# One matmul of 512 queries per value head instead of two of 256, and a new order of TensorE's work in the attention step

## What is computed

```python
Q = (x @ Wq).reshape(B, S, NUM_HEADS, 2 * HEAD_DIM).transpose(0, 2, 1, 3)
K = (x @ Wk).reshape(B, S, NUM_HEADS, 2 * HEAD_DIM).transpose(0, 2, 1, 3)
V = (x @ Wv).reshape(B, S, NUM_HEADS, HEAD_DIM).transpose(0, 2, 1, 3)
Q1, Q2 = jnp.split(Q, 2, axis=-1)
K1, K2 = jnp.split(K, 2, axis=-1)
A1 = jnp.einsum('bhqd,bhkd->bhqk', Q1, K1) * scaling
A2 = jnp.einsum('bhqd,bhkd->bhqk', Q2, K2) * scaling
attn = jax.nn.softmax(A1, axis=-1) - lamb * jax.nn.softmax(A2, axis=-1)
out = jnp.einsum('bhqk,bhkd->bhqd', attn, V)
```

## Time and profile before

| | us |
|---|---|
| median of three runs | 3233.75 (3232.12 to 3233.81) |
| span of the profiled execution | 3232.2 |
| TensorE busy | 3089.3 |
| VectorE busy | 2735.8 |
| ScalarE busy | 2502.6 |
| attention steps with all three kinds of work | 193.8 to 2487.7 |

### The profile page before, as it was taken

The page is one execution under the profiler, slowest core; times in us unless marked ns, Lnnn a source line. Parts: engine busy times, 40 slices in busy tenths (PEclk is TensorE's granted clock), DMA queues, the critical chain, the costliest instruction groups (busy, mean ns, idle before and its releaser), DMA issues. The chain is left out here.

```text
span 3232.2 us, 72457 instructions
## 1 busy us (share of the span) xinstructions
PE 3089.3 (96%) x29281; PEld 1389.4 (43%) x29282; DVE 2735.8 (85%) x2902; ACT 2502.6 (77%) x4689; POOL 453.2 (14%) x654
## 2 busy tenths in 40 slices
PE   8999999999999999999999999999999969999995
PEld 4333333333333333333333333333332658999995
DVE  3599999999999999999999999999998683433443
ACT  3269999999999999999999999999999552333333
POOL 2000000000000000000000000000000464555554
PEclk9989999999999999999999999999999979999997
DMA  6520101111020101011010101021002561222224
GB/s 159 124 45 15 35 21 30 30 34 28 15 35 24 28 15 35 29 30 28 28 28 18 34 21 28 15 51 28 15 9 83 206 227 34 38 38 36 36 37 124
DMA packets 101213, 152.92 MB, mean 47 GB/s; under 512 B 21592, under 2 KB 64464, under 8 KB 99248
## 3 DMA queue, kind: packets, MB, share of 16 engines
q1 hardware_dynamic: 85008, 130.03, 16.2%
q0 software_dynamic: 15904, 18.66, 3.6%
HBM read 88.35 MB, written 60.29 MB: 46 GB/s over the span
## 5 line engine op out<-in xcount | busy, mean ns | idle before, releaser
L1005 DVE TENSOR_REDUCE half_max<-scores 128x2 f32<-128x1024 f32 x2016 | 2297.4, 1219 | 10.5 <-PE scores L759 4.8
L930 ACT ACTIVATE probs<-bank 128x512 f32<-128x512 f32 x4012 | 2142.3, 595 | 142.5 <-PE bank L772 45.5
L831 PE MATMUL bank<-probs,V 128*32 128x256 f32 x16384 | 1309.6, 391 | 44.2 <-ACT probs L930 42.4
L759 PE MATMUL scores<-K,Q 48*128 48x512 f16 x4032 | 793.9, 388 | 3.0 <-SPq L542 2.2
L772 PE MATMUL bank<-Q,K 50*128 50x512 f16 x4012 | 789.7, 380 | 0.0
L831 PEld LDWEIGHTS bank<-probs,V 128*32 128x32 f32 x16384 | 322.5, 108 | 583.2 <-issue 517.7
L759 PEld LDWEIGHTS scores<-K,Q 48*128 48x128 f16 x4032 | 194.2, 93 | 834.6 <-DVE half_max L1005 532.2
L772 PEld LDWEIGHTS bank<-Q,K 50*128 50x128 f16 x4012 | 371.2, 94 | 183.0 <-ACT probs L930 4.2
L660 POOL TENSOR_SCALAR max_parts<-row_max 128x16 f16<-128x16 f32 x64 | 16.2, 253 | 2066.3 <-DVE row_max L1011 2066.3
L1604 ACT ACTIVATE h<-u 128x1024 f32<-128x1024 f32 x71 | 75.0, 1057 | 260.8 <-DVE u L1648 260.8
L1565 PE MATMUL pre<-xgT,w 128*128 128x128 f32 x2272 | 265.3, 275 | 2.3 <-ACT xgT L1598 2.3
(11 more groups left out here) (195 smaller groups left out, 1204.8 us busy)
## 6 DMA issues: line engine op xcount, KB each, us to landing
attended<-att SPq DMA_DIRECT2D x64, 256.0 KB, 2.5
W<-in_L_ffn_w_dram SPq DMA_DIRECT2D x16, 1024.0 KB, 6.4
Q<-q_parts SPq DMA_DIRECT2D x96, 128.0 KB, 6.6
K<-k_parts SPq DMA_DIRECT2D x96, 128.0 KB, 6.9
values<-attended SPq DMA_DIRECT2D x6, 2048.0 KB, 9.2
q_parts<-parts SPq DMA_DIRECT2D x64, 128.0 KB, 2.4
k_parts<-parts SPq DMA_DIRECT2D x64, 128.0 KB, 2.4
xT<-in_x_cols_dram SPq DMA_DIRECT2D x8, 512.0 KB, 4.9
```

The source lines that it names most:

```text
L759: mm = nc.tensor.matmul(scores[:, b, h, :], Q[p][r, c, up, t * P:(t + 1) * P], K[p][r, up, kc * TC:(kc + 1) * TC], start=True, stop=True)
L831: mm = nc.tensor.matmul(banks[att_bank[s // KB]][32 * u:32 * u + 32, q], V[wp][:, wk, u // 2, :], probs[:, 4 * s % RING + u, q], start=(wk ...
L930: nc.scalar.activation(probs[:, i % RING, :], banks[tile_bank[i]][:], ACT.Exp, scale=SCALE).then_inc(exp_done, 1)
L1005: nc.vector.tensor_reduce(half_max[lc % 2][:, :, up, t, kc], scores[:, b], AX.X, ALU.max).then_inc(max_done[b], 1)
```

## The change

`weigh` loses its two parts: each of the four units is one matmul of 512 queries, and all four stand in one block per step. With them go the second reading of the values and the start flag's tie to part 0. The waits ahead of the block are the same. In each half of the step the transposed pair now stands ahead of the maxima pair. The order per step becomes: transposed pair 0, maxima pair 0, value matmuls, transposed pair 1, maxima pair 1.

```diff
-                        def weigh(s, part):
+                        def weigh(s):
 
                             wp, wk = s // KB // CH, s % KB
...
                             for u in range(UNITS):
-                                q = slice(TC // 2 * part, TC // 2 * (part + 1))
-                                mm = nc.tensor.matmul(banks[att_bank[s // KB]][32 * u:32 * u + 32, q], V[wp][:, wk, u // 2, :],
-                                                      probs[:, 4 * s % RING + u, q],
-                                                      start=(wk == 0 and part == 0), stop=(wk == KB - 1), skip_group_check=True)
-                            if part == 1:
-                                mm.then_inc(pv_done, 1)
+                                mm = nc.tensor.matmul(banks[att_bank[s // KB]][32 * u:32 * u + 32, :], V[wp][:, wk, u // 2, :],
+                                                      probs[:, 4 * s % RING + u, :],
+                                                      start=(wk == 0), stop=(wk == KB - 1), skip_group_check=True)
+                            mm.then_inc(pv_done, 1)
...
-                        weigh(j, 0)
+                        transposed(it, j, lc, 0)
                         if item < STEPS:
                             score_pair(item, ahead // KB, ahead % KB * 2)
-                        transposed(it, j, lc, 0)
-                        weigh(j, 1)
+                        weigh(j)
+                        transposed(it, j, lc, 1)
                         if item < STEPS:
                             score_pair(item, ahead // KB, ahead % KB * 2 + 1)
-                        transposed(it, j, lc, 1)
```

More of the change, by code:

```diff
@@ L817, in _ @@
                             pe.wait_ge(max_loaded[(lc + 1) % 2], MXD * (it * CH + (lc + 1) // 2 + 1) + 1)
-                        def weigh(s, part):
+                        def weigh(s):
                             wp, wk = s // KB // CH, s % KB
[L822 to L828, removed]
-                            for u in range(UNITS):
-                                q = slice(TC // 2 * part, TC // 2 * (part + 1))
-                                mm = nc.tensor.matmul(banks[att_bank[s // KB]][32 * u:32 * u + 32, q], V[wp][:, wk, u // 2, :],
-                                                      probs[:, 4 * s % RING + u, q],
-                                                      start=(wk == 0 and part == 0), stop=(wk == KB - 1), skip_group_check=True)
-                            if part == 1:
-                                mm.then_inc(pv_done, 1)
+                            if wk == 0:
+                                pe.wait_ge(exp_done, it * 4 * RS + att_after[s // KB] + 1)
+                            else:
+                                pe.wait_ge(exp_done, it * 4 * RS + 4 * s + 4)
+                            if s % (CH * KB) == 0:
+                                pe.wait_ge(v_copied, 2 * it + wp + 1)
+                            for u in range(UNITS):
+                                mm = nc.tensor.matmul(banks[att_bank[s // KB]][32 * u:32 * u + 32, :], V[wp][:, wk, u // 2, :],
+                                                      probs[:, 4 * s % RING + u, :],
+                                                      start=(wk == 0), stop=(wk == KB - 1), skip_group_check=True)
+                            mm.then_inc(pv_done, 1)
                         if it * RS + j == SETUP_AT:
```

## The result

The changed kernel takes 3584.13 us (median of four runs, 3580.73 to 3585.14) against 3233.15 before (four runs, the three of the table ahead and one more): 1.1085 times as long, 95% interval 1.1070 to 1.1101. The forecast was 3565 us, range 3505 to 3640. Its profiled execution spans 3581.2 us.

What follows compares the result with a forecast made beforehand. VectorE's reductions bound the kernel, TensorE and a ScalarE loop within one per cent. After the change 939 steps of 2.59 us and 62 of 3.09 make 2623.6 against 2294; with +1, 3233.75 + 331 = 3565 us, range 3505 to 3640.

Steps and rivals of the forecast that it cites:

- T0: First pair of transposed-score matmuls of a step, tiles 0 and 1; its second matmul was forecast to wait for an exponential.
- T1: Second pair of transposed-score matmuls of a step, tiles 2 and 3.
- that ring: Loop through ScalarE: T1, tile 2's exponential, the next T0's second matmul, S0, W, T1 again; forecast 2.59 us per step.
- S0: First pair of matmuls for the maxima in a step, forecast to queue behind T0's waiting matmul.
- Term (a): Value matmuls merged to 512 columns: W goes from 0.57 us per half to 1.00 us, bounds 0.97 and 1.14.
- W: The value matmuls of a step on TensorE, 256 columns in each half before, 512 in one block after.
- Term (b): New order: the loop through ScalarE sets the step at 2.59 us, though TensorE's own sum falls from 2.24 to 1.97.
- Term (c): First step of a chunk: T0 waits for the exponential of the tile just before it, so the step takes 3.09 us.
- No change: Rival 1: VectorE stays the bound, 3233 us or down to 3223; chance 8%.
- Slower still: Rival 2: W of 512 columns costs 1.14 us, the loop 2.73, 3705 us in all; chance 8%.
- The granted clock: Rival 3: TensorE's clock falls because it waits in every step; half the clock gives over 4500 us; chance 2%.
- S's waits: Waits of the maxima matmuls for VectorE, forecast as met because a reduction ends long before its bank is written again.

Runs made afterwards that it cites:

- kernels 3: Changed kernel with maxima pair 0 put ahead of transposed pair 0: 3364.88 us, 1.0409 against the kernel before.
- kernel 4: Changed kernel with the exponential of tile 2 of each step on 128 of its 512 columns: 3262.27 us, 1.0089 against the kernel before.
- kernel 5: Changed kernel with the exponential of tile 1 of each step on 128 of its 512 columns: 3582.64 us, 1.1078 against the kernel before.
- kernel 2: Changed kernel with the merge alone, value matmuls in one block at the step's start, maxima pairs ahead of transposed pairs: 3658.78 us, 1.1317 against the kernel before.
- kernel 7: Changed kernel with the exponential of tile 2 of each step on 32 of its 512 columns: 3238.97 us, 1.0016 against the kernel before.
- kernel 1: Kernel before with the new order alone, value matmuls still in two halves, transposed pairs ahead of maxima pairs: 3222.66 us, 0.9968 against the kernel before.
- kernel 6: Changed kernel with maxima pair 0 ahead of transposed pair 0 and tile 2's exponential on 128 of 512 columns: 3267.88 us, 1.0107 against the kernel before.

## Why the prediction was right

- **Where the time would be set.** The step that decided was to leave TensorE's sum (which fell, 1280.6 to 1070.5 us in the value matmuls) and to follow the second matmul of T0 back to the exponential of T1's first tile. The timeline after and kernels 3, 4 and 5 show that ring, each by another of its members: S0 (0.22 us of it), the exponential of tile 2, and tile 1 as the one that is not in it.
- **Term (a)**, W of 512 queries at 1.00 us: measured 1202.15 to 1203.15, 1.00. Two matmul instructions of 0.43 leave 0.14, the same rest as W of 256 had, now once per step. The Trainium skill's rule on the drain at a change of tiling mode (TensorEngine Tiling (Array Packing), Key Properties) agrees with a saving of this kind; no run here tells a drain from another fixed cost, and the saving bought nothing.
- **Term (b)**, the step at 2.59: measured 2.61. T1 to its exponential took 0.42 (0.41 in the sum), and by the time the second matmul of T0 started 1.08 had passed (1.06); T0 to W was 0.53, as summed. The copies' distance gives the step to a third digit, (42.22 - 3.10)/15 = 2.608; 0.018 us in each of 939 steps and 0.01 in each of 62 make 17.5 of the 19 us between 3565 and 3584. The lower of the two delays in the trace of before, 0.03, was the right one to take: it is 0.03 again (1200.54 + 0.39 to 1200.96), while tile 0 has its 0.09 again in kernel 2 (1200.81 + 0.38 to 1201.28).
- **Term (c)**, the chunk's first step at 3.09: measured 3.10. The low end of the range, where this is hidden, didn't come about.
- **VectorE's idle time**, forecast at some 330 us: the groups show 263.3, but its busy time rose by 85.0 (2280.7 to 2365.7) at the same count and nearly the same mean, since of the reductions, which used to overlap by 0.09 us, only the two of a pair still do (2.36 us for two). Both together are 338 more than before.
- **The rivals.** No change (8%) needed the ring to be shorter by 0.33 us. Kernel 7 shows the point: with the exponential of tile 2 shortened by 0.40 the time comes within 0.2% of before. Slower still (W at 1.14) fell with term (a). The granted clock stayed at 1.00 in the stretch:

```profile
193.00:2834.00 2641.00, 2344.68 (x16012) 472.62 (x16008) 2378.79 (x2125) 2102.34 (x4064) 69.26 (x208) 1.00 0.11 24
```

(193 to 2834 us: length, busy us of PE, PEld, DVE, ACT and POOL with instructions, granted clock, DMA share, GB/s.)
- **What it overlooked.** It priced the two parts together and never the order alone, which is a gain of 0.32%. It also took VectorE's chunk for 36.6 us, with 0.4 for the row maxima: kernel 1 shows 36.42, so that 0.26 is left beside 32 x 1.13, and the rest of the 36.6 was waiting at the chunk's start. And it took S's waits as met once and for all: that holds in the changed order, but the same sum for kernel 6 missed the second ring.

## What to carry to other kernels

Where engines hand tiles round a ring of few buffers, a longer block on one engine isn't priced by that engine's sum: go once round each ring (matmul, exponential, release, the queue behind the released matmul, the long block) and take the longest, and after one ring is cut, sum the next one before expecting the full gain. A saving on an engine that doesn't set the pace brought nothing here, while the even spacing of its short pieces may be what keeps the others busy. In an engine that works in order, put what is ready ahead of what may have to wait: one swap of two neighbours moved this kernel by 219 us.

## What the runs showed of the hardware

- An exponential takes 0.597 us on 512 columns (kernel 5), 0.278 on 128 (kernel 4) and 0.197 on 32 (kernel 7), so some 0.83 ns per column and 0.17 us that stay. Shortening a tile saves less than its share.
- VectorE can lose time that isn't shown as idle: a reduction lasts 1.22 us, but the next one can start 1.13 us after it. In kernel 6 (193 to 2520 us) the idle time ahead of its reductions was 14.9 us, and the kernel was 45 us slower than kernel 1:

```profile
L1002 DVE TENSOR_REDUCE half_max<-scores 128x2 f32<-128x1024 f32 x2002 | 2308.3, 1217 | 14.9 <-PE scores L759 3.0
```

The idle time is 11.4 us more than in kernel 1 and the busy time 33.0 more: together 44.4.
